# Vision tower on one core: last batch reordered, router logits taken from centred tokens, products with unread results ahead of waits of TensorE

## The chip, the cores and the metric

The kernel runs on one NeuronCore of a Trainium2 chip. The core has a matrix engine (TensorE, PE in the rows), a vector engine (VectorE, DVE), an activation engine (ScalarE, ACT), a general engine (GpSimd, POOL) and a queue for transfers (SyncE, SP). The metric is the device time of one execution in microseconds, the median over several runs.

## What is computed

Eight images of 64 channels x 128 steps x 64 variables pass one transformer layer. All numbers are float32.

```python
h = tok_ref(x, W)                      # rfft of patches, product: (8, 1024, 64)
h = concatenate([cls_tok, h], axis=1)  # one class token ahead of 1024 tokens
h = h + attn(layernorm(h), WQ, WK, WV) # causal softmax attention, head size 64
h = h + ffn(layernorm(h), ...)

def ffn(x, Wr, br, ...):
    feat = mean(x, axis=0)             # over the EIGHT images
    w = softmax(feat @ Wr + br)        # weights of 8 experts for each token place
    h = relu(bn(x @ W1[e] + b1)); h = relu(bn(h @ W2[e] + b2))
    y = h @ Wo[e] + bo                 # three products for each expert
    return sum over e of w[e] * y[e]
```

The layernorm of the second half is (x - mean) / sqrt(var + eps) without gain or offset: a centred token times one number, its rstd. Because the router takes the mean over all eight images, no expert result can be weighted before the last image has passed the attention.

## The kernel before

Batches (images) 0 to 7 go through a software pipeline; every engine has its own program, written out by hand, and semaphores tie them. The order of instructions in each program is the order of the code. Within a batch the attention works on eight tiles of 128 queries. For each tile PE makes the scores (`score`, into the two PSUM banks pairs `Sp[0]`, `Sp[1]`), DVE takes the row minimum of the negated scores (`smax`), ACT the exponential (`expo`), POOL cuts the triangle (`tri`), DVE masks and sums (`mask`), PE transposes (`p_turn`, into `PTB`, whose halves are `PTp[0]` and `PTp[1]`), ACT copies to SBUF (`pt_copy`, semaphore `pt_done`), and PE multiplies with the values (`u_group`, `u_last`, then `o_group` with `WVT`, in the pair `MM`, halves `M0` and `M1`). Batch 7 runs its tiles downwards, 7 to 0.

The tokens' second layernorm is `ln2_centre`, `ln2_sq`, `ln2_ss`, `ln2_rstd`, `ln2_e` for batches 0 to 6 and `last_add`, `last_centre`, `last_sq`, `last_ss`, a rstd on POOL (L569, L571) and `last_e` in two halves A and B for batch 7. `e2_turn` transposes the result and `e2t_copy` brings it to `E2T`, semaphore `e2t_done`. `facc` is the sum of E2T over batches 0 to 6.

`layer1(n)` is the first expert product of pair p = n % 4 of experts in batch n // 4: four products of 64x512. ACT reads it with `h1_wide(n)` (semaphore `h1_done`). There are 32 of them. Numbers 0 and 1 are made in batch 6, numbers 2 to 11 inside the last batch, the rest in the last phase. Those below `NMID` use `PTB`, so that transposes must wait until `h1_wide` has read them; the others alternate between `Sp[0]` and `Sp[1]`.

Behind `layer1(9)` stands the router: facc times `WrB` (L1778), the class token (L1779), E2T of batch 7 times `WrB` (L1785), then on DVE the logits, maximum, difference, on ACT the exponential, on DVE the sum and weights (L1202 to L1228). The class token has a chain of its own (`class_max`, `class_weight`, `class_h`, `class_centre`, `class_ss`, `class_rstd`, then L1768, L1769, L1773 and L1792 on PE). After that comes the last phase: `layer2`, the gating on DVE, `layer3`, `turn_out`, store, batch after batch, from about 288 us to the end.

## Time and profile before

| | us |
|---|---|
| median of 3 runs | 383.86 (382.93 to 384.4) |
| profiled execution, device time | 382.6 |
| its span, first to last instruction | 380.9 |
| PE busy | 356.5 (94% of the span) |
| DVE busy | 270.7 (71%) |
| ACT busy | 199.7 (52%) |
| POOL busy | 133.5 (35%) |
| mean granted TensorE clock | 0.963 of full |

Busy shares alone name PE as the engine to look at. [...] A row of a list in order of time gives the start, the length, the engine, the line of the kernel and the operation with its tiles, count, and in brackets the idle time before it with what ended it. Each float32 product of TensorE appears as two matmul records, each transpose as one; a line's count is of records.

### The profile page before, as it was taken

To read this page: it belongs to the slowest core of one execution; us is meant where nothing else is said; L and a number is where in the kernel's file an instruction comes from. 1 tells how busy PE (TensorE), PEld (TensorE's weight loads), DVE (VectorE), ACT (ScalarE), POOL (GpSimd) and SP (SyncE) were. 2 spreads that over 40 slices of the span, in tenths; PEclk is the share of its full clock that TensorE was granted. 3 is DMA by queue.
4 is the path that set the end of the run, shared out by engine and by line. 5 is a ranking of instruction groups with operands and counts; after the bars stand their busy time and mean duration, and the time that the engine had idled before them with its cause. 6 is when DMAs were issued, how large, how long until landed. Compare 5 with 4: busy or idle time off the path is not lost.

```text
span 380.9 us, 7929 instructions
## 1 busy us (share of the span) xinstructions
PE 356.5 (94%) x2682; PEld 170.9 (45%) x2682; DVE 270.7 (71%) x582; ACT 199.7 (52%) x402; POOL 133.5 (35%) x201
## 2 busy tenths in 40 slices
PE   4889999999999999999999987897999999999985
PEld 2565335356356355355357444352564333333331
DVE  3122867889989989989999989676315566766673
ACT  0224656568468478377387686664535344444410
POOL 7051302525625626626627538315302900000000
PEclk9999999999999999999999999896559999999999
DMA  6999741904605505500000000000000011100112
GB/s 154 224 219 186 147 79 37 186 0 98 128 0 109 113 0 118 102 0 0 2 2 3 0 2 1 2 0 2 1 0 3 2 28 29 29 12 18 29 28 57
DMA packets 28991, 20.44 MB, mean 54 GB/s; under 512 B 12280, under 2 KB 28832, under 8 KB 28960
## 3 DMA queue, kind: packets, MB, share of 16 engines
q1 hardware_dynamic: 28352, 19.91, 25.8%
q8 instruction: 19, 0.31, 0.4%
q10 hardware_dynamic: 608, 0.12, 0.2%
q14 instruction: 12, 0.10, 0.1%
HBM read 17.93 MB, written 2.10 MB: 53 GB/s over the span
## 4 chain that ended last, share of the span: by engine, by line
PE 82%; DVE 5%; issue 4%; ACT 4%; POOL 2%; DMA 1%; SPq 0%; DVEq 0%; POOLq 0%; ACTq 0%
PE Sp L1406 13%; PE Sp L1553 8%; PE MM L1461 6%; PE MM L1687 6%; PE PTB L1418 6%; PE PTB L1665 6%; PE MM L1339 6%; PE MM L1342 5%; PE MM L1469 2%; PE MM L1316 2%; PE Sp L1288 2%; PE MM L1320 2%; PE PTB L1388 1%; POOL st L479 1%; PE Sp L1707 1%
## 5 line engine op out<-in xcount | busy, mean ns | idle before, releaser
L1406 PE MATMUL Sp<-eT,G 64*64 64x512 f32 x512 | 63.7, 599 | 0.2 <-issue 0.2
L449 POOL TENSOR_SCALAR_AFFINE_SELECT EP<-EP 128x128 f32<-128x128 f32 x64 | 23.6, 368 | 103.1 <-ACT EP L654 103.0
L591 ACT ACTIVATE PT<-PTB 128x512 f32<-128x512 f32 (+3 forms) x88 | 38.9, 484 | 26.4 <-PE PTB L1418 23.8
L945 DVE TENSOR_SCALAR_CACHE_REDUCE EP<-Sp,sr 128x1024 f32<-128x1024 f32 x32 | 40.3, 1279 | 5.6 <-PE Sp L1406 5.6
L945 DVE TENSOR_SCALAR_CACHE_REDUCE SN<-Sp,sr 128x1024 f32<-128x1024 f32 x32 | 39.9, 1276 | 1.2 <-PE Sp L1406 1.2
L1406 PEld LDWEIGHTS Sp<-eT,G 64*64 64x64 f32 x512 | 18.8, 133 | 31.4 <-issue 31.2
L1553 PE MATMUL Sp<-E2T,W1f 64*64 64x512 f32 x216 | 31.8, 688 | 0.1
L1461 PE MATMUL MM<-PT,e 128*64 128x512 f32 (+3 forms) x168 | 31.6, 513 | 0.0
L955 DVE SCALAR_TENSOR_TENSOR SN<-SN,EP 128x384 f32<-128x384 f32 (+7 forms) x32 | 27.4, 855 | 4.4 <-ACT EP L657 2.3
L1237 DVE SCALAR_TENSOR_TENSOR EP<-PTB,negc,PTd 128x512 f32<-128x512 f32 x28 | 19.7, 746 | 13.3 <-PE PTB L1665 13.3
L955 DVE SCALAR_TENSOR_TENSOR EP<-EP 128x128 f32<-128x128 f32 (+7 forms) x32 | 27.3, 853 | 2.2 <-ACT EP L657 1.9
L657 ACT ACTIVATE EP<-SN,negm 128x256 f32<-128x256 f32 (+6 forms) x31 | 23.3, 751 | 0.0
L1461 PEld LDWEIGHTS MM<-PT,e 128*64 128x64 f32 x168 | 14.9, 141 | 18.5 <-issue 16.3
L1418 PE MATMUL PTB<-ident,SN 128*128 128x128 f32 x146 | 20.6, 280 | 1.9 <-ACT X L699 1.4
L1418 PEld LDWEIGHTS PTB<-ident,SN 128*128 128x128 f32 x146 | 16.3, 144 | 10.3 <-issue 5.6
L1418 PE MATMUL PTB<-ident,EP 128*128 128x128 f32 x106 | 16.1, 283 | 2.7 <-ACT PTd L591 2.6
L1418 PEld LDWEIGHTS PTB<-ident,EP 128*128 128x128 f32 x106 | 11.4, 142 | 13.8 <-issue 11.2
L591 ACT ACTIVATE UT<-MM 128x512 f32<-128x512 f32 x12 | 7.1, 589 | 18.9 <-PE MM L1687 15.0
L654 ACT ACTIVATE EP<-SN,negm 128x128 f32<-128x128 f32 x32 | 12.8, 400 | 7.6 <-DVE SN L945 7.4
L591 ACT ACTIVATE Z<-MM 128x512 f32<-128x512 f32 x11 | 6.6, 597 | 19.3 <-PE MM L1687 11.7
L657 ACT ACTIVATE EP<-EP,negm 128x128 f32<-128x128 f32 (+6 forms) x25 | 16.6, 662 | 0.0
L479 POOL TENSOR_TENSOR st<-st,cst 128x8 f32<-128x8 f32 x7 | 15.5, 2211 | 1.3 <-POOL st L476 1.3
(334 smaller groups left out, 699.3 us busy)
## 6 DMA issues: line engine op xcount, KB each, us to landing
XW<-in_x_dram SPq DMA_DIRECT2D x6, 1024.0 KB, 10.7
X<-in_x_dram SPq DMA_DIRECT2D x6, 1024.0 KB, 9.5
out_dram<-xc SPq DMA_DIRECT2D x8, 256.0 KB, 2.6
XW<-in_x_dram SPq DMA_DIRECT2D x2, 576.0 KB, 7.9
X<-in_x_dram SPq DMA_DIRECT2D x2, 576.0 KB, 14.2
XW<-in_x_dram SPq DMA_DIRECT2D x2, 448.0 KB, 11.2
X<-in_x_dram SPq DMA_DIRECT2D x2, 448.0 KB, 14.2
EP<-in_L_tok_W_dram SPq DMA_DIRECT2D x2, 144.0 KB, 3.3
```

Of the source, the lines that this page charges most:

```text
L449: pool.affine_select(out=blk_, in_=blk_, compare_op=ALU.is_ge, fill=0.0, base=0, pattern=[[-1, 128]], channel_multiplier=1).then_inc(tri_d ...
L591: return act.activation(dst, src, ACT.Copy)
L657: act.activation(EP[:, p % 2, 0:n], W4[p % 4][:, 0:n], ACT.Exp, bias=negm[q][:, t:t + 1], scale=-1.0).then_inc(left_done, 1)
L945: dve.tensor_scalar(W4[p % 4], Sp[p % 2][:, :], -SCALE, sr[q][:, place(t), 0:1], ALU.mult, ALU.min, accum_out=negm[q][:, t:t + 1]).then_in ...
L955: dve.scalar_tensor_tensor(out=W4[p % 4][:, 0:n], in0=W4[p % 4][:, 0:n], scalar=0.0, in1=EP[:, p % 2, 0:n], op0=ALU.not_equal, op1=ALU.mul ...
L1339: pe.matmul(M0[64 * c:64 * c + 64, :], Wef[:, n, 0, :], X[q][:, :, n, vs], start=(n == 0), stop=False, skip_group_check=True)
L1406: ins = pe.matmul(Sp[p % 2][64 * s:64 * s + 64, CH * c:CH * c + CH], G[q][rows, 128 * t + 64 * s:128 * t + 64 * s + 64], eT[q][rows, :], **ON)
L1418: ins = pe.transpose(PTp[i % 2][:, 128 * k:128 * k + 128], W4[p % 4][:, 128 * (k0 + k):128 * (k0 + k) + 128], ident[:, :])
L1461: ins = pe.matmul(M1[half, q0:CH], e32[q][:, place(k), :], PT[g][:, k, q0:CH], start=(k < 2), stop=(k >= nk - 2), skip_group_check=True)
L1553: ins = pe.matmul(l1_bank(n)[64 * s:64 * s + 64, CH * c:CH * c + CH], W1f[rows, 128 * p + 64 * s:128 * p + 64 * s + 64], E2T[rows, b, :], ...
L1665: ins = pe.matmul(l2_bank(b, p)[c][half:half + 64, :], W2f[rows, p, :], h1[b % 4][rows, c, p, :], **ON)
L1687: ins = pe.matmul(yP[b // (NB - 1)][h][64 * c:64 * c + 64, :], Wof[rows, 2 * j + c, :], t2[b % 2][2 * j + c][rows, :], start=(j == 0), sto ...
```

## The change

1. `keep_up(bank, n)` is new: one product of the 128x128 identity with n columns of E2T, written to a bank whose content is not needed. Nothing reads it. It is called five times: 256 columns in batch 6 between `e_turn_early` and `g_quarters`, 512 in the last batch between `p_turn(b, 0)` and `p_turn(b, 1)`, 512 ahead of the wait for the class token's e2c, 256 ahead of the wait of `e2_turn(b - 1)`, and 384 ahead of the wait for facc.
2. `NMID` goes from 5 to 4: `layer1(4)` is written to `Sp[0]` instead of `PTB`. It waits for `smax` of piece 6 in exchange, since that reads the bank.
3. The program of PE in the last batch: `score` of pieces 6 and 7 ahead of `layer1(3)`; `p_turn` 6 and 7 together ahead of `layer1(5)`; `u_last` both in a row; `layer1(6)` ahead of the layernorm work.
4. The router's logits of batch 7 are made from the centred tokens `xc`: `x_turn` transposes them in two halves (4 transposes together), ACT copies them to `XT` (the tile eT[1]), PE multiplies with `WrB`, and DVE multiplies the 128x64 result with the rstd (`glx`) before it adds. The normalised tokens of batch 7, needed for `layer1(28)` and later only, are made after the logits (`last_e`), transposed by `last_turn` in the last phase behind `layer3(0, 2)`, and copied by ACT after `h1_wide(12)`. `layer1(13)` waits for that copy, since the bank is shared.
5. DVE: `class_arg` and `smax` 6 and 7 come earlier; `ln2_centre(6)` moves from ahead of `mask` 5 to behind `class_centre`, `class_ss` ahead of `last_add` A; `ln2_ss` and `ln2_e` of batch 6 move behind halves A and B; `h1c` of the class token moves ahead of the addition to facc. ACT and POOL follow: `expo` 2, 6 and 7 earlier, `ln2_sq` later, `pt_copy` 6 and 7 ahead of `h1_wide(4)`, `add_up` of half A behind the last `tri`, `class_rstd` ahead of `ln2_rstd`.

PE, from the second product of half A's outputs (UT) to the last product with unnormalised weights. PTB, Sp0, Sp1 and MM are PSUM, SN is the tile with masked exponentials. Before:

```order
L1553 MATMUL PTB<-E2T,W1f 64x512 [waits pt_done,e2t_done]
L1553 MATMUL PTB<-E2T,W1f 64x512 x3
L1418 MATMUL PTB<-ident,SN 128x128 [waits pt_done,p_done,h1_done]
L1418 MATMUL PTB<-ident,SN 128x128
L1553 MATMUL Sp1<-E2T,W1f 64x512 [waits h1_done,e2t_done,negm_done]
L1553 MATMUL Sp1<-E2T,W1f 64x512 x3
L1437 MATMUL MM<-PT0,e32_1 64x384 [waits dve_steps,pt_done]
L1437 MATMUL MM<-PT0,e32_1 64x384
L1437 MATMUL MM<-PT0,e32_1 64x256
L1437 MATMUL MM<-PT0,e32_1 64x128
L1418 MATMUL PTB<-ident,SN 128x128 [waits pt_done,p_done]
L1437 MATMUL Sp0<-PT0,e32_1 64x128 [waits pt_done]
```

After:

```order
L1564 MATMUL Sp0<-E2T,W1f 64x512 [waits h1_done,e2t_done,negm_done]
L1564 MATMUL Sp0<-E2T,W1f 64x512 x3
L1429 MATMUL PTB<-ident,SN 128x128 [waits pt_done,p_done]
L1429 MATMUL PTB<-ident,SN 128x128
L1429 MATMUL PTB<-ident,SN 128x128 [waits pt_done,p_done]
L1448 MATMUL MM<-PT0,e32_1 64x384 [waits dve_steps,pt_done]
L1448 MATMUL MM<-PT0,e32_1 64x384
L1448 MATMUL MM<-PT0,e32_1 64x256
L1448 MATMUL MM<-PT0,e32_1 64x128
L1448 MATMUL PTB<-PT0,e32_1 64x128 [waits pt_done]
L1564 MATMUL Sp1<-E2T,W1f 64x512 [waits h1_done,e2t_done,negm_done]
L1564 MATMUL Sp1<-E2T,W1f 64x512 x3
```

`layer1(4)` (E2T,W1f) left PTB, the transposes behind it lost the wait for h1_done, and both transposes now stand ahead of `u_last` and of `layer1(5)`.

PE, from the class token's first products to the router's last one. Before:

```order
L1773 MATMUL PTB<-e2cT,W1f 128x8 [waits act_steps]
L1773 MATMUL PTB<-e2cT,W1f 128x8 x3
L1553 MATMUL Sp0<-E2T,W1f 64x512 [waits h1_done,e2t_done]
L1553 MATMUL Sp0<-E2T,W1f 64x512 x3
L1778 MATMUL MM<-WrB,facc 128x16 [waits facc_done]
L1778 MATMUL MM<-WrB,facc 128x16 x3
L1779 MATMUL MM<-WrB,f64 128x8
L1477 MATMUL MM<-ident,e32_0 128x128 [waits e2_done]
L1477 MATMUL MM<-ident,e32_0 128x128 x3
L1553 MATMUL Sp1<-E2T,W1f 64x512 [waits h1_done,e2t_done]
L1553 MATMUL Sp1<-E2T,W1f 64x512 x3
L1785 MATMUL MM<-WrB,E2T 128x16 [waits dve_steps,e2t_done]
```

After:

```order
L1406 MATMUL MM<-E2T,ident 128x256
L1488 MATMUL MM<-ident,e232 128x128 [waits e2_done]
L1488 MATMUL MM<-ident,e232 128x128 x3
L1564 MATMUL Sp0<-E2T,W1f 64x512 [waits h1_done,e2t_done]
L1564 MATMUL Sp0<-E2T,W1f 64x512 x3
L1406 MATMUL PTB<-E2T,ident 128x384
L1807 MATMUL PTB<-WrB,facc 128x16 [waits facc_done]
L1807 MATMUL PTB<-WrB,facc 128x16 x3
L1808 MATMUL PTB<-WrB,f64 128x8
L1811 MATMUL MM<-WrB,eT1 128x16 [waits act_steps]
L1811 MATMUL MM<-WrB,eT1 128x16 x3
L1564 MATMUL Sp1<-E2T,W1f 64x512 [waits h1_done,e2t_done]
```

In front of the router stand now products of 256 and of 384 columns whose results are not read, and the transposes of batch 6 (e232). The transposes of batch 7 (e32_0) are gone from here, and the router's second product reads eT1. The transposes of xc stand ahead of these rows, two before the class token's L1796 and two behind it.

PE, in the last batch between the first two groups of transposes. After:

```order
L1429 MATMUL PTB<-ident,EP 128x128 [waits pt_done,p_done]
L1429 MATMUL PTB<-ident,EP 128x128 x3
L1429 MATMUL PTB<-ident,EP 128x128 [waits pt_done,p_done]
L1429 MATMUL PTB<-ident,EP 128x128 x3
L1406 MATMUL MM<-E2T,ident 128x512 [waits e2t_done]
L1429 MATMUL PTB<-ident,EP 128x128 [waits pt_done,p_done]
```

Before, the same rows follow each other without the one from L1406.

```diff
@@ names and steps
+        glx = sb("glx", [128, NT * NEXP])
...
+        XT = eT[1]
...
-        NMID = 5
+        NMID = 4
@@ GpSimd, last_batch
                 tri(b, 5, True)
-                add_up(b, 1, pz, 0)
                 tri(b, 6, True)
                 tri(b, 7, True)
-                ln2_rstd(b - 1)
+                add_up(b, 1, pz, 0)
                 class_h()
                 add_up(b, 0, pzl, 1)
+                class_rstd()
+                ln2_rstd(b - 1)
...
@@ ScalarE, last batch
             pt_copy(b, 0, True)
+            expo(b, 1, 2, True)
             pt_copy(b, 1, True)
-            expo(b, 1, 2, True)
             expo(b, 1, 3, True)
...
+            expo(b, 1, 6, True)
             h1_wide(3)
-
-            ln2_sq(b - 1)
+            expo(b, 1, 7, True)
...
+            pt_copy(b, 6, True)
+            pt_copy(b, 7, True)
             h1_wide(4)
-
-            pt_copy(b, 6, True)
+            act.wait_ge(dve_steps, nth("k_cent", 1))
+            act.activation(e2c[:, :], ccx[:, :], ACT.Square).then_inc(act_steps, 1)
             act.wait_ge(pe_steps, nth("t_ua", 1))
             copy(U2[0][:, 128:CH], M0[:, 128:CH]).then_inc(act_steps, 1)
-            pt_copy(b, 7, True)
             act.wait_ge(pe_steps, nth("t_ub", 1))
-            copy(U2[0][0:64, 0:128], Sp[0][0:64, 0:128]).then_inc(act_steps, 1)
+            copy(U2[0][0:64, 0:128], PTp[0][0:64, 0:128]).then_inc(act_steps, 1)
+            ln2_sq(b - 1)
             h1_wide(5)
...
+            h1_wide(6)
+            act.wait_ge(pe_steps, nth("q_x7", 1))
+            copy(XT[:, 2 * 128:CH], M1[:, 2 * 128:CH]).then_inc(act_steps, 1)
+            last_sq("B", slice(0, QG))
+            act.wait_ge(pe_steps, nth("q_x7", 2))
+            copy(XT[:, 0:2 * 128], M1[:, 0:2 * 128]).then_inc(act_steps, 1)
+            e2t_copy(b - 1, M0)
             h1_wide(7)
             h1_wide(8)
-            e2t_copy(b, M1)
             h1_wide(9)
...
             h1_wide(12)
+            e2t_copy(NB - 1, Sp[1])
@@ VectorE, last batch
+            dve.wait_ge(pool_steps, nth("t_rstdB", 1))
             dve.wait_ge(pe_steps, nth("q_lg", 1))
+            dve.tensor_tensor(glx[:, :].rearrange("p (i c e) -> p i c e", i=QG, c=2),
+                              M1[:, 0:64].rearrange("p (c i e) -> p i c e", i=QG, c=2),
+                              st[:, 3, :].rearrange("p (c i) -> p i c", c=2).unsqueeze(3).to_broadcast([128, QG, 2, NEXP]),
+                              ALU.mult).then_inc(dve_steps, 1)
...
+            last_e(1, A).then_inc(dve_steps, 1)
+            last_e(0, B).then_inc(e2_done, 1)
             dve.wait_ge(pe_steps, nth("c_l2", 1))
@@ TensorE
+            def keep_up(bank, n):
+
+                pe.matmul(bank[:, 0:n], ident[:, :], E2T[:, 0, 0:n], **ON)
...
                 if n == 13:
-                    pe.wait_ge(act_steps, nth("q_bcc", 4))
+                    pe.wait_ge(e2t_done, NB)
...
                 e_turn_early(b + 1, 1 - q)
+                if not y_next:
+                    pe.wait_ge(pt_done, NCH * b + 4)
+                    keep_up(PTp[0], 256)
...
             p_turn(b, 0, paired=True, down=True)
+            pe.wait_ge(e2t_done, b - 1)
+            keep_up(M0, CH)
             p_turn(b, 1, paired=True, down=True)
...
+            def x_turn(x, bank, first, last):
+                for i in range(first, last):
+                    ins = pe.transpose(bank[:, 128 * i:128 * i + 128], x[:, 2 * i:2 * i + 2, :], ident[:, :])
+                ins.then_inc(pe_steps, 1)
+
+            layer1(6)
             pe.wait_ge(dve_steps, nth("t_hA", QG))
-            e2_turn(b - 1, M1)
-            pe.wait_ge(dve_steps, nth("t_hB", QG))
-            layer1(6)
+            keep_up(M1, CH)
             pe.wait_ge(dve_steps, nth("k_e2", 1))
...
             layer1(7)
+            pe.wait_ge(dve_steps, nth("t_hA", QG))
+            x_turn(xc, M1, 2, QG)
             pe.wait_ge(act_steps, nth("q_cmc", 1))
...
+            x_turn(xc, M1, 0, 2)
+            keep_up(M0, 256)
+            e2_turn(b - 1, M0)
             layer1(8)
+            keep_up(PTp[0], 384)
             pe.wait_ge(facc_done, NB)
...
-            e2_turn(b, M1, e2=e32[0])
+            pe.wait_ge(act_steps, nth("q_x7c", 2))
+            for i in range(QG):
+                ins = pe.matmul(M1[:, 16 * i:16 * i + 16], XT[:, 128 * i:128 * i + 128], WrB[:, :], **ON)
+            ins.then_inc(pe_steps, 1)
             layer1(9)
...
                 layer3(b - 1, 2)
+                if b == 1:
+                    last_turn()
                 layer3(b - 1, 3)
```

## Rows read from the trace of the kernel before

**Rows 1.** Page: span, busy time, granted clock in tenths, in 40 slices
```profile
span 380.9 us, 7929 instructions
...
PE 356.5 (94%) x2682; PEld 170.9 (45%) x2682; DVE 270.7 (71%) x582; ACT 199.7 (52%) x402; POOL 133.5 (35%) x201
...
PEclk9999999999999999999999999896559999999999
```

**Rows 2.** Windows: length, busy us of each engine (records), granted clock, DMA, GB/s
```profile
core 0: us, PE busy (x) PEld busy (x) DVE busy (x) ACT busy (x) POOL busy (x), PEclk, DMA share, GB/s
240.15:243.56 3.41, 3.41 (x10) 0.97 (x12) 2.10 (x9) 2.54 (x6) 1.05 (x2) 0.50 0.02 5
260.62:284.52 23.90, 22.98 (x93) 11.17 (x93) 7.90 (x38) 8.99 (x17) 6.61 (x11) 0.50 0.00 1
284.52:288.40 3.88, 3.88 (x47) 2.23 (x46) 1.75 (x10) 2.63 (x4) 0.29 (x1) 1.00 0.02 4
288.40:380.90 92.50, 86.08 (x730) 29.45 (x728) 55.30 (x83) 33.69 (x36) 11.27 (x17) 1.00 0.11 24
```

**Rows 3.** PE in order of time, around the beginnings of two stretches
```profile
235.40 1.09 PE L1418 MATMUL PTB<-ident,EP 128*128 128x128 f32 x8
239.14 1.01 PE L1418 MATMUL PTB<-ident,EP 128*128 128x128 f32 x7 [2.65 <-ACT PTd L591]
...
257.00 1.06 PE L1743 MATMUL MM<-WVT,UT 128*128 128x64 f32 x8
258.57 1.09 PE L1553 MATMUL PTB<-E2T,W1f 64*64 64x512 f32 x8 [0.51 <-ACT PT L591]
261.04 0.69 PE L1418 MATMUL PTB<-ident,SN 128*128 128x128 f32 x2 [1.37 <-ACT X L699]
```

**Rows 4.** PE in order of time, 266 to 284 us
```profile
266.74 0.69 PE L1437 MATMUL Sp<-PT,e 128*64 128x128 f32 x2 [0.37 <-ACT PT L591]
...
270.30 1.99 PE L1553 MATMUL Sp<-E2T,W1f 64*64 64x512 f32 x8
...
274.98 1.87 PE L1773 MATMUL PTB<-e2cT,W1f 64*128 64x8 f32 x8
...
278.69 1.89 PE L1778 MATMUL MM<-WrB,facc 128*128 128x16 f32 x8
...
281.03 1.11 PE L1477 MATMUL MM<-ident,e 128*128 128x128 f32 x4
282.07 1.99 PE L1553 MATMUL Sp<-E2T,W1f 64*64 64x512 f32 x8
```

**Rows 5.** PE in order of time at full clock, elsewhere in the trace
```profile
197.04 0.95 PE L1394 MATMUL MM<-agT,eT 128*128 128x4 f32 x8
...
206.44 0.60 PE L1477 MATMUL Sp<-ident,e 128*128 128x128 f32 x4
...
220.04 1.09 PE L1388 MATMUL PTB<-eT,A 64*64 64x512 f32 x8 [0.88 <-ACT eT L591]
...
370.37 0.66 PE L1697 MATMUL MM<-ident,UT 128*128 128x128 f32 x4 [1.24 <-DVE UT L1242]
...
371.97 3.66 PE L1680 MATMUL Sp<-EP,Wof 128*64 128x512 f32 x16
```

**Rows 6.** DVE and POOL in order of time, batch 7's tokens to logits
```profile
269.01 0.28 DVE L1134 SCALAR_TENSOR_TENSOR H<-MM,pzl,H 128x64 f32<-128x64 f32 x1 [4.01 <-PE MM L1759]
...
277.43 0.42 DVE L1140 TENSOR_TENSOR e<-xc,st 128x256 f32<-128x256 f32 x1
...
285.33 0.22 DVE L1208 SCALAR_TENSOR_TENSOR gl<-MM,gl 128x64 f32<-128x64 f32 x1 [3.96 <-PE MM L1785]
...
274.31 1.01 POOL L571 TENSOR_TENSOR st<-st,cst 128x4 f32<-128x4 f32 x1
```

More of the change, by code:

```diff
@@ L1168, in _ @@
             class_centre()
+            ln2_centre(b - 1)
+            class_ss()
             dve.wait_ge(pvs_done, 2 * b + 1)
@@ L1180, in _ @@
                 last_add(t, pzl, M0[:, D * t:D * t + D])
+            dve.wait_ge(pe_steps, nth("t_ob", 1))
+            last_add(0, pzl, PTp[1][:, 0:D])
             last_ss("A", A)
[L1182 to L1183 removed]
             dve.wait_ge(dve_steps, nth("t_hB", QG))
             last_centre("B", B)
[L1186 removed]
+            ln2_e(b - 1)
             last_ss("B", B)
[L1188 to L1193 removed]
             dve.wait_ge(pe_steps, nth("c_l1", 1))
@@ L1722, in _ @@
             p_turn(b, 3, paired=True, down=True)
+            score(b, 1, 6, True)
             pe.wait_ge(r0_done, NB)
@@ L1744, in _ @@
             ins.then_inc(o_ready, 1)
-            layer1(4, NCH * b + 10)
-            pe.wait_ge(h1_done, 10)
+            pe.wait_ge(negm_done, 8 * NB - 1)
+            layer1(4)
             p_turn(b, 6, paired=True, down=True)
-            pe.wait_ge(negm_done, 8 * NB)
-            layer1(5)
+            p_turn(b, 7, paired=True, down=True)
             pe.wait_ge(pt_done, NCH * b + 11)
@@ L1753, in _ @@
             u_last(QG, M0, 128)
-            p_turn(b, 7, paired=True, down=True)
             pe.wait_ge(pt_done, NCH * NB)
-            u_last(1, Sp[0], 0)
+            u_last(1, PTp[0], 0)
+            pe.wait_ge(negm_done, 8 * NB)
+            layer1(5)
             pe.wait_ge(act_steps, nth("t_uac", 1))
@@ L1825, in _, with last_turn @@
             layer3(0, 1)
+            def last_turn():
+                pe.wait_ge(act_steps, nth("q_bcc", 4))
+                pe.wait_ge(e2_done, NB)
+                for i in range(QG):
+                    ins = pe.transpose(L1p[1][0][:, 128 * i:128 * i + 128], e32[0][:, 2 * i:2 * i + 2, :], ident[:, :])
+                ins.then_inc(e2t_ready, 1)
             for b in range(1, NB):
```

82 lines of the change are left out of this document (32 added, 50 removed).

## The prediction

> **What bounds the kernel now.** I read three views in this order. The page first [rows 1]: PE is busy 94% of the span, so time is won where PE works slowly or stands still. The row of the granted clock names the place: it is full nearly everywhere and falls to 6, 5, 5 tenths near the end of the attention. [...] In the long stretch it was busy 22.98 of 23.90 us while DVE was busy 7.90, ACT 8.99 and POOL 6.61. So this stretch is bound by PE at half clock. From 288.40 to the end PE is busy 86.08 of 92.50 us at full clock, and this last phase begins only when the router is through: what PE reaches sooner in the stretch, the end reaches sooner.
>
> The list in order of time shows what PE did before each fall [rows 3]. Before the first it stood idle 2.65 us between two groups of transposes. Before the second it had 1.06 us of products with 64 columns, 0.51 us idle, one `layer1` of 1.09 us, and 1.37 us idle. PE then fed on little for long: the class token's products with 8 columns (1.87 us) and the router's with 16 (1.89 us), with `layer1` between them [rows 4]. The clock came back only at 284.5, behind transposes and a `layer1` in a row.
>
> **Does half the clock mean twice the time?** The same work stands in the trace at both clocks. `layer1` takes 1.99 us [rows 4]; the four 64x512 products of L1388 take 1.09 with the drain of the last one [rows 5]. Four transposes take 1.11 against 0.60, four products with few columns 1.89 against 0.95 [rows 4, 5]. So work scales by about two, idle time does not. At full clock the busy part of the stretch would be 22.98 / 2 = 11.5 us: a saving of 11.5. [...]
>
> **The long stretch, part by part.**
> - Waits. `layer1(4)` no longer waits for a half of PTB (0.51), `p_turn(6)` no longer for `h1_wide(4)` (1.37) [rows 3], and `u_last` of one tile no longer for a lone copy (0.37) [rows 4]: 2.25 us. In exchange `p_turn` 6 and 7 now stand back to back ahead of `u_last`, which needs the copy of the first; nothing covers that copy but one transpose. I leave 0.5 us for it. Gain 1.75, bounds 1.2 and 2.2. That these waits go is the first reason for the clock to stay: the 1.9 us idle of [rows 3] shrink to some 0.5.
> - Products with unread results, three in this region: 512 + 256 + 384 = 1152 columns. The nearest row is L1680 with 128 rows: 8 products of 512 columns, two at a time, in 3.66 us [rows 5], so 0.91 for one that fills the array. 1152 / 512 x 0.91 = 2.1 us at full clock. Do they lie in waits? If PE runs at full clock and is behind, they do not: from the additions of half A (about 262) e2c needs some 1.5 us of DVE and POOL, while PE has `u_last`, two `layer1` and the outputs, over 4 us, ahead of it; the copy of E2T that facc needs has `layer1(8)` as cover. I take the whole 2.1 as cost; bound below 0.5, if the chains are slower than I think.
> - Router from centred tokens. New: four transposes (0.60 [rows 5]) and two small copies on ACT, which has the time. The four transposes of the normalised tokens leave this stretch and come back in the last phase at the same 0.6, where PE has no gap at that place. Net cost 0.6. The dependency that this shortens (POOL's rstd ended at 275.3, `last_e` waited behind the class token until 277.43, the logits' addition came at 285.33 [rows 6]) was not the limit: DVE stood waiting for PE 3.96 us before it. At full clock it would be one, and this edit takes it away; that is its worth, and it is inside the halving above.
> - DVE: one more operation of the size of the additions to the logits (0.22 us [rows 6]), behind `layer1(9)` and two more; hidden. `last_e` moved behind the logits adds 0.84 us of DVE before the weights. The exponential on ACT and PE's `layer1` 10, 11 and `layer2` cover it: cost 0, and at most 0.4.
> - `ln2_centre(6)` (1.6 us) now sits between `class_centre` and the additions of half A on DVE. The half-B products of PE, which DVE waited for by 4.01 us [rows 6], come later than that work even at full clock. Cost 0; up to 1 if DVE runs late.
>
> Sum: -11.5 - 1.75 + 2.1 + 0.6 = -10.6 us.
>
> **The rest.** The 512-column product at 236.5 lies in the 2.65 us of idle [rows 3] and the 256-column one in the 0.88 us before L1388 [rows 5]: both wait there for ACT, so they cost nothing as time. Their worth is the first fall. It slowed 3.41 us of busy PE, so 1.7 us are to be had, since scores come next and DVE waits for them. The idle left is 2.65 - 0.9 = 1.75 us. Gaps of 0.88 and 1.24 us left the clock at full [rows 5], 1.37 + 0.51 with little work between ended in a fall. The value lies between 0 and 1.7; 1.75 is nearer the fall, but it is now preceded by a dense product. I take 0.8. The move of `score` 6 and 7 ahead of `layer1(3)` changes the order, not the sum, and feeds DVE sooner.
>
> Total -11.4. The profiled execution took 382.6, 1.3 below the median of 383.86, so it would give 371.2 and the median 383.86 - 11.4 = **372.5 us**.
>
> **Rivals.**
> 1. *The clock falls again for a short time.* The router's products (facc, class token, batch 7) now follow each other: 0.95 + 0.3 + 0.95 us with 8 or 16 columns, then one `layer1`, then the class token's second product. It is the thinnest place of the new order, and in the old trace the clock did not come back over just such work. For it: the old fall came with thin products plus idle; against: here no idle is left. One fall like that at 240.15 costs 1.7 us, two 3.4: 374.2 to 375.9.
> 2. *The clock falls at the class token's products and stays down until after the router.* Between `layer1(7)` and `layer1(9)` lie about 6.3 us of work at full clock with the two unread products; at half it takes 12.6. That gives 378.8. [...]
> 3. *DVE, ACT or POOL becomes the bound.* At full clock PE is 11 us faster and the layernorm chain of batch 7 with 1.6 us of `ln2_centre` ahead is next. If it leaves PE waiting some 3 us in all, partly in place of the unread products: 375.5.
> 4. *The clock does not hold at all (the slower side).* The fall at 260.6 comes in spite of shorter waits, and the unread products run at half clock: 2 x 2.1 = 4.2, the new transposes 1.1, one set of transposes moves to full clock (-0.5), waits -1.75. Sum +3.0: 386.9. With a share f of the stretch at full clock the change wins 11.5 f - 2.7 (2 - f) + 1.75; it turns to a loss below about f = 0.26.
>
> **How the numbers follow.** Forecast, long stretch gone and the first fall gone or not (371.6 to 373.4, with the bounds of waits and unread products 370 to 374.5): 0.57. Rival 1: 0.17. Rival 2: 0.10. Rival 3: 0.06. Rival 4: 0.10. The range goes from 370.0 to 378.0; it takes in rivals 1 and 3 and leaves out 2 and 4. A measurement of this kernel can tell about 0.5% (1.9 us) from no change. Faster by more: all but rival 4 and a tail of rival 2, 0.88. Within: 0.03, the tails of both. Slower: 0.09, the rest of rival 4.
>
> **What would show it.** The granted clock at 1.00 from 244 us to the end; `layer1` 5 to 9 at about 1.1 us each instead of 1.99; no wait of PE for `h1_wide` between 257 and 262; the gating of batch 0 beginning about 10 us sooner; the distance from there to the end longer by 0.6. If the clock is at 0.50 for more than 4 us behind 257, rival 1, 2 or 4 holds, by its length. If the clock is full and PE waits more than 1 us at L1788 or L1807 of the new kernel, rival 3. Wrong altogether would be a stretch at full clock without a shorter time to the last phase.

## The result, and the profile after

The changed kernel takes **371.29 us** (median of 4 runs, 369.55 to 373.43) beside 384.13 us of the kernel before in the same set (382.93 to 384.67). The ratio is 0.967, 95% interval 0.962 to 0.973: 12.8 us less by the medians. Ratios here and below leave out executions more than 1.5% above the fastest of the same kernel; medians leave out none. The profiled execution took 371.4 us against 382.6, 11.2 us less.

The page of the changed kernel: span, busy time, and the granted clock in 40 slices.

```profile
span 369.6 us, 7961 instructions
...
PE 348.3 (94%) x2696; PEld 167.9 (45%) x2696; DVE 270.8 (73%) x583; ACT 199.9 (54%) x404; POOL 132.8 (36%) x201
...
PEclk9999999999999999999999999999999999999999
```

Against [rows 1], the 6, 5, 5 in the row of the clock are gone. PE's busy share is 94% as before, at a mean granted clock of 1.000 where it was 0.963: the busy share did not show the clock, the row below it does. DVE, ACT and POOL did the same work in both.

The windows of the changed kernel, cut so that each answers to one of [rows 2] (columns as there). Its pair of 240.15:243.56 stands at nearly the same place; 256.20:277.50 holds what took half the clock before; the last begins behind the router.

```profile
240.15:243.56 3.41, 3.41 (x23) 1.47 (x25) 2.95 (x10) 2.65 (x6) 1.51 (x3) 1.00 0.02 5
256.20:277.50 21.30, 20.43 (x162) 10.71 (x161) 12.39 (x55) 14.00 (x26) 7.70 (x14) 1.00 0.01 2
277.50:369.60 92.10, 86.03 (x727) 29.41 (x727) 55.03 (x83) 33.18 (x36) 11.27 (x17) 1.00 0.11 24
```

In the first window PE has 23 matmul records where it had 10 before, in the same 3.41 us, busy throughout in both; some of the 23 are shorter ones of the work behind `u_group`.

PE in order of time, from batch 6 to the first transposes of the outputs in the last phase; these answer to [rows 3 to 5]. L1406 is `keep_up`, L1564 `layer1`, L1429 the transposes, L1472 `u_group`, L1826 the transposes of the weights, with which the last phase begins.

```profile
197.09 0.95 PE L1401 MATMUL MM<-agT,eT 128*128 128x4 f32 x8
...
236.38 1.02 PE L1406 MATMUL MM<-E2T,ident 128*128 128x512 f32 x2
239.19 1.01 PE L1429 MATMUL PTB<-ident,EP 128*128 128x128 f32 x7 [1.79 <-ACT PTd L593]
240.13 3.01 PE L1472 MATMUL MM<-PT,e 128*64 128x512 f32 x16
...
255.62 1.06 PE L1759 MATMUL MM<-WVT,UT 128*128 128x64 f32 x8
256.61 1.09 PE L1564 MATMUL Sp<-E2T,W1f 64*64 64x512 f32 x8
257.63 0.55 PE L1429 MATMUL PTB<-ident,SN 128*128 128x128 f32 x3
258.54 1.08 PE L1448 MATMUL MM<-PT,e 128*64 128x384 f32 x7 [0.36 <-ACT PT L593]
...
262.84 1.12 PE L1406 MATMUL MM<-E2T,ident 128*128 128x512 f32 x2
...
265.76 1.05 PE L1796 MATMUL PTB<-e2cT,W1f 64*128 64x8 f32 x8
...
267.02 0.60 PE L1406 MATMUL MM<-E2T,ident 128*128 128x256 f32 x2
267.45 0.60 PE L1488 MATMUL MM<-ident,e 128*128 128x128 f32 x4
...
269.00 0.91 PE L1406 MATMUL PTB<-E2T,ident 128*128 128x384 f32 x2
269.75 0.96 PE L1807 MATMUL PTB<-WrB,facc 128*128 128x16 f32 x8
...
276.40 0.66 PE L1826 MATMUL MM<-ident,gwp 128*128 128x128 f32 x4
...
296.81 0.66 PE L1711 MATMUL MM<-ident,UT 128*128 128x128 f32 x4
```

The idle time ahead of the first fall is 1.79 us where it was 2.65, and `u_group` behind it takes 3.01 us. `layer1(4)` waits for nothing. Up to 277.5 us two waits are left, 0.36 us for the copy of `p_turn` and 0.17 us ahead of `layer1(11)`; a `layer1` takes 1.09 us. The class token's 8-column products take 1.05 instead of 1.87, facc's 16-column ones 0.96 instead of 1.89.

Before going on, one reading of the numbers that all runs share. Each execution comes with its mean granted clock. A time multiplied by that clock is about the time with the loss at half speed taken off. An execution with a share s at half clock has the mean 1 - s/2 (before: 27.31 us [rows 2] and 0.8 us at the end, of 380.9, give 0.963), and it loses about s/2 of its time if all of its work takes twice as long there (`layer1` 1.99 us against 1.09). It is an estimate, since it counts idle time at half clock as lost too, and it scatters: over 12 executions of the changed kernel it gives 369.3 to 371.7 us. The kernel before, 33 executions in three sets: medians of 369.7, 370.0 and 370.3 us. The changed kernel, those 12 executions in two sets: 370.6 and 370.4 us. **By this estimate the two kernels would take the same time at full clock, within 1 us.** What the change gained is the clock. What it saved in waits (1.9 us) it spent on unread products (2.0) and on item 4 (0.8), as the runs below show.

### The profile page after: what moved, and what is told of

Same layout as the page of the kernel before. It is cut to its first block, busy times and chain, and to the rows that moved or that the text cites. A ratio compares the mean times of both kernels' runs of the same rounds, so it can differ in the third digit from the quotient of the medians.

```text
span 369.6 us, 7961 instructions
## 1 busy us (share of the span) xinstructions
PE 348.3 (94%) x2696; PEld 167.9 (45%) x2696; DVE 270.8 (73%) x583; ACT 199.9 (54%) x404; POOL 132.8 (36%) x201
## 4 chain that ended last, share of the span: by engine, by line
PE 80%; DVE 4%; issue 4%; DMA 4%; ACT 3%; POOL 2%; SPq 1%; DVEq 0%; POOLq 0%; ACTq 0%
PE Sp L1417 13%; PE Sp L1564 7%; PE MM L1701 7%; PE PTB L1679 7%; PE PTB L1429 6%; PE MM L1472 6%; PE MM L1346 6%; PE MM L1349 5%; DMA XW<-in_x_dram 4%; PE MM L1480 3%; PE MM L1323 2%; PE PTB L1395 1%; PE MM L1327 1%; POOL st L481 1%; PE Sp L1721 1%
## 5 line engine op out<-in xcount | busy, mean ns | idle before, releaser
L1472 PE MATMUL MM<-PT,e 128*64 128x512 f32 (+3 forms) x168 | 29.9, 491 | 0.0
L1564 PE MATMUL Sp<-E2T,W1f 64*64 64x512 f32 x224 | 28.6, 602 | 0.2 <-ACT XW L701 0.2
L1472 PEld LDWEIGHTS MM<-PT,e 128*64 128x64 f32 x168 | 14.5, 137 | 17.2 <-issue 15.1
L1429 PE MATMUL PTB<-ident,SN 128*128 128x128 f32 x146 | 19.9, 277 | 0.6 <-ACT PTd L593 0.6
L1429 PEld LDWEIGHTS PTB<-ident,SN 128*128 128x128 f32 x146 | 16.2, 143 | 8.1 <-issue 5.6
L1429 PE MATMUL PTB<-ident,EP 128*128 128x128 f32 x106 | 16.1, 282 | 1.9 <-ACT PTd L593 1.8
L656 ACT ACTIVATE EP<-SN,negm 128x128 f32<-128x128 f32 x32 | 12.8, 401 | 9.1 <-DVE SN L950 7.4
L1429 PEld LDWEIGHTS PTB<-ident,EP 128*128 128x128 f32 x106 | 11.4, 142 | 13.5 <-issue 10.9
L469 POOL TENSOR_TENSOR H<-H,ot 128x256 f32 (+1 forms) x14 | 14.0, 997 | 3.2 <-DVE ot L990 1.9
```

The source lines that it names most:

```text
L1429: ins = pe.transpose(PTp[i % 2][:, 128 * k:128 * k + 128], W4[p % 4][:, 128 * (k0 + k):128 * (k0 + k) + 128], ident[:, :])
L1472: ins = pe.matmul(M1[half, q0:CH], e32[q][:, place(k), :], PT[g][:, k, q0:CH], start=(k < 2), stop=(k >= nk - 2), skip_group_check=True)
L1564: ins = pe.matmul(l1_bank(n)[64 * s:64 * s + 64, CH * c:CH * c + CH], W1f[rows, 128 * p + 64 * s:128 * p + 64 * s + 64], E2T[rows, b, :], ...
```

## The experiments

Twelve runs of ten different kernels stand in three sets, each set on one chip beside 11 executions of the kernel before. Times are medians (lowest to highest); the mean granted clock of the executions is given as a range, with the number of executions at 0.995 or less. Above that, the end of the span alone can account for what lacks: the profiled execution of `layer1(4)` in PTB, at 0.996, has the full clock to 366 us and half from 366.8 to 369.6. At 0.995 I take it as open: the profiled execution without all five has 3.41 us at half, at 241.01, and none at its end.

| kernel | us | clock of its executions | 0.995 or less |
|---|---|---|---|
| set 1: before | 383.42 (380.77 to 387.13) | 0.958 to 0.972 | 11 of 11 |
| changed kernel | 370.93 (370.21 to 373.55) | 0.990 to 1.000 | 1 of 6 |
| without product of the gap | 373.46 (371.46 to 374.35) | 0.988 to 0.993 | 6 of 6 |
| without the late three | 371.29 (368.24 to 371.78) | 0.988 to 1.000 | 4 of 6 |
| without all five | 371.95 (370.44 to 374.18) | 0.979 to 0.995 | 6 of 6 |
| set 2: before | 381.72 (380.67 to 386.89) | 0.958 to 0.972 | 11 of 11 |
| before + product of the gap | 379.65 (372.15 to 384.41) | 0.963 to 0.999 | 5 of 6 |
| before + all five | 375.6 (373.29 to 380.31) | 0.975 to 0.997 | 5 of 6 |
| router from normalised tokens | 369.6 (369.08 to 370.34) | 0.996 to 1.000 | 0 of 6 |
| thin products apart | 369.95 (368.08 to 373.6) | 0.983 to 0.998 | 3 of 6 |
| set 3: before | 380.95 (376.15 to 385.1) | 0.962 to 0.985 | 11 of 11 |
| changed kernel | 371.84 (370.02 to 375.49) | 0.984 to 1.000 | 3 of 6 |
| `layer1(4)` in PTB | 374.32 (371.27 to 376.45) | 0.986 to 0.997 | 4 of 6 |
| router from normalised tokens | 369.95 (369.43 to 372.08) | 0.995 to 0.999 | 1 of 6 |
| the same, two products less | 370.35 (368.59 to 374.79) | 0.986 to 1.000 | 3 of 6 |

**My theory** after the result: the order with its shorter waits ends the long stretch at half clock, the product in the gap ends the short one, and the late products are the price of holding the clock over the router. **The rivals**: the unread products do it all, the order nothing; the order does it all, the products nothing; and the shorter chain over rstd has a part in it.

### Changed kernel again

> The changed kernel as it is, as the yardstick for the three that are run with it on the same chip. Expected 371.3 us (369.5 to 373.5), 12 to 13 below the kernel before, the granted clock at 1.00 from 12 us to the last product.

370.93 us, ratio 0.970 (0.965 to 0.974). In set 3 it stood beside a faster kernel before:

> The changed kernel without an edit, as the yardstick of this set of runs. 371 us (369.6 to 373.6 in the runs so far), TensorE's granted clock at full from 11 us to the end, its waits behind 250 us 0.4 (p_turns on ScalarE), 0.6 (l1_turn on ScalarE) and 0.2 us.

371.84 us, ratio 0.979 (0.974 to 0.984). The profiled execution was the slowest of its six, 375.49 us. Three windows of it, of two stretches at half clock and of the one ahead of the second:

```profile
33.85:40.67 6.82, 6.82 (x32) 3.09 (x27) 2.85 (x6) 1.22 (x6) 0.29 (x1) 0.50 0.72 117
272.77:276.19 3.42, 3.42 (x45) 2.78 (x48) 1.43 (x7) 1.13 (x2) 0.00 (x0) 1.00 0.02 5
276.19:279.61 3.42, 3.42 (x22) 1.46 (x18) 1.46 (x9) 2.30 (x3) 0.29 (x1) 0.50 0.01 2
```

So the clock can still fall in the changed kernel, in some executions. By distances between the same instructions in the traces of this run and of the result, the first stretch cost 3.2 us (12.00 against 8.80 around it) and the second 1.3 (22.08 against 20.78 from the products of UT to the weights), together 4.5; 375.49 - 4.5 = 371.0, where the executions at clock 1.0 have 371.33 and 371.37. The second fall stands out: PE was busy 3.42 of 3.42 us ahead of it, with the router's products of 16 and 8 columns, those of the class token and a `layer1`.

### Without the product in the gap

```diff
-            pe.wait_ge(e2t_done, b - 1)
-            keep_up(M0, CH)
```

> The changed kernel without the 512-column product between the first two groups of transposes of the last batch; all else stays. Theory 1 (that product alone keeps the clock over the gap at 237 us): the idle time there goes back from 1.79 to 2.65 us, the clock falls for about 3.4 us as in the kernel before, +1.7 us against the changed kernel, some 373.0. Rival (the clock stays because the neighbouring work is arranged otherwise): no fall, same time as the changed kernel within 0.3 us. Both expect the clock at 1.00 from 256 us on.

373.46 us against 370.93. PE around the gap, and the window behind it:

```profile
239.47 1.01 PE L1429 MATMUL PTB<-ident,EP 128*128 128x128 f32 x7 [2.64 <-ACT PTd L593]
240.41 4.71 PE L1472 MATMUL MM<-PT,e 128*64 128x512 f32 x16
```

```profile
240.45:243.86 3.41, 3.41 (x9) 0.96 (x10) 2.94 (x10) 2.27 (x5) 1.52 (x3) 0.50 0.02 5
```

The idle time is 2.64 us again, and `u_group` takes 4.71 us. All six executions have a clock below 0.994, which fits a fall every time; the place of it is seen in the profiled one. One product of 512 columns, in time in which PE waited anyway, removed it. By the trace it is worth 4.71 - 3.01 = 1.7 us; by the medians 2.5, with ranges that allow either.

### Without the three late products

```diff
-            keep_up(M1, CH)
-            keep_up(M0, 256)
-            keep_up(PTp[0], 384)
```

> The changed kernel without the three unread products (512, 256, 384 columns) behind layer1(6), ahead of the transposes of batch 6 and ahead of the product with facc. Theory 1 (the reordering and the shorter waits hold the clock, the three products are pure cost): clock at 1.00 throughout, PE reaches the last phase 1.9 us sooner, some 369.4. Theory 2 (they are needed at the thin place): the clock falls once or for long between 265 and 275 us, +1.7 to +6 minus the 1.9 saved, so 371 to 375. Theory 3 (they lie in waits of PE anyway): clock full, but new waits of together 1 to 2 us, time unchanged.

371.29 us, ratio 0.967 (0.962 to 0.971), against 370.93, 0.970: no difference that can be told. But the six times fall apart: two at clock 1.0 took 368.24 and 368.59, three at 0.988 took 371.71 to 371.78. The profiled execution is of the second kind. PE in order of time, and the window:

```profile
267.13 1.07 PE L1804 MATMUL PTB<-WrB,facc 128*128 128x16 f32 x8 [0.40 <-DVE facc L1202]
...
268.44 1.21 PE L1808 MATMUL MM<-WrB,eT 128*128 128x16 f32 x8
269.58 1.99 PE L1564 MATMUL Sp<-E2T,W1f 64*64 64x512 f32 x8
```

```profile
269.22:276.05 6.83, 6.83 (x47) 3.42 (x50) 2.74 (x13) 2.65 (x4) 0.29 (x1) 0.50 0.00 1
```

This is my rival 1, at the place that it named: facc, class token and batch 7 in a row, and the clock falls in the third group. It costs 6.83 / 2 = 3.4 us. With the products that fall is avoided and they cost about 2.2. The two come out even in the median. Fewer executions lack clock with the products (1 of 6 against 4 of 6), but the times are no steadier: both kernels' times spread over some 3.4 us. The clock fell behind 2.65 us of idle at the first gap before, and here at 269.22 with no wait longer than 0.40 us near it: short gaps alone did not protect it.

### Without all five unread products

> The changed kernel without any of the five unread products. If their effects add up: the first fall is back (+1.7) and the rest as in the run without the three late ones: with theory 1 there 371.1, with theory 2 there 373 to 377. If the clock falls at 260 us for as long as in the kernel before, it is the products and not the order that held it: 380 or more.

371.95 us, ratio 0.972 (0.967 to 0.977). The diff is the sum of the two before and the 256-column product of batch 6. The windows of its first fall and of the old long stretch's work:

```profile
241.01:244.42 3.41, 3.41 (x11) 1.04 (x9) 2.58 (x10) 1.91 (x5) 1.51 (x2) 0.50 0.02 5
256.20:277.50 21.30, 20.37 (x174) 11.51 (x170) 13.48 (x65) 15.16 (x28) 9.29 (x16) 1.00 0.01 2
```

So the new order, with the router from centred tokens, is enough to end the long stretch in this execution, and by the medians it brings about 11.5 of the 12.5 us that the whole change won in this set. The other clocks go down to 0.979, so some executions had further time at half, at places that no trace shows.

### The old order with the product in the gap

> The kernel before with one thing added: the unread product of 512 columns between the first two groups of transposes of the last batch. Theory (it alone holds the clock over that gap): no fall at 240 us, the long fall at 260 us as before but beginning and ending 1.7 us sooner; 383.4 - 1.7 = 381.7 us. If the effect needed the rest of the change: the fall stays, 383.4.

379.65 us against 381.72 by the medians, 2.1 less where 1.7 was expected; with single executions 12 us apart that proves little, and the trace has to carry it. `keep_up` was added to the kernel before, with one call. Its profiled execution (381.24 us) has no fall at 240, as the theory says, and the long one is cut in two:

```profile
258.83:262.24 3.41, 3.41 (x15) 0.90 (x16) 2.53 (x14) 0.37 (x1) 1.93 (x5) 0.50 0.00 0
262.24:269.07 6.83, 4.33 (x34) 2.30 (x34) 3.40 (x16) 4.61 (x10) 1.58 (x4) 1.00 0.00 1
269.07:286.14 17.07, 17.07 (x90) 10.01 (x90) 3.31 (x16) 5.96 (x8) 2.49 (x4) 0.50 0.00 1
```

The clock came back, PE then waited 2.5 of 6.83 us, and it fell again, for 17.07 us with PE busy all the time. The fall begins 4.52 us behind the start of the products of UT (254.31 here), where in the kernel before it is 3.62 (260.62 - 257.00 in [rows 2, 3]); PE's instructions from there on are the same. The executions of this one kernel reach from 372.15 us at 0.999 to 384.41 at 0.963. So the length of the long fall is no property of the order alone. Whether the edit 20 us earlier moved it in the profiled execution, or something that differs from execution to execution, cannot be told from one trace of each.

### The old order with all five products

```diff
+                if not y_next:
+                    pe.wait_ge(pt_done, NCH * b + 4)
+                    keep_up(PTp[0], 256)
...
+            pe.wait_ge(e2t_done, b - 1)
+            keep_up(M0, CH)
...
+            keep_up(M1, 256)
             e2_turn(b - 1, M1)
...
+            keep_up(M0, CH)
             pe.wait_ge(dve_steps, nth("k_e2", 1))
...
+            keep_up(M0, 384)
             pe.wait_ge(facc_done, NB)
```

> The kernel before in its own order, with five unread products: 256 columns in batch 6 and 512 in the first gap as in the change, and 256 ahead of the transposes of batch 6, 512 ahead of the class token's products, 384 ahead of facc. Theory 1 (the long fall comes from PE's waits of 0.51 and 1.37 us, which stand ahead of the late products): the fall at about 259 us stays, the late products run at half clock (+4.1), the first gap gives -1.7: 385.8 us. Theory 2 (more dense work lets the clock come back sooner in the stretch): the stretch at 0.50 is some 7 us shorter, 380 to 382.

375.6 us, ratio 0.982 (0.977 to 0.986). Theory 1 of this run, that the fall stays long, is wrong in the profiled execution and by the clocks of four more; one, at 0.975 and 380.31 us, is near the kernel before. PE at the waits that the new order removes and at the first of the late products, and the windows:

```profile
259.02 1.09 PE L1557 MATMUL PTB<-E2T,W1f 64*64 64x512 f32 x8 [0.52 <-ACT PT L591]
261.48 0.44 PE L1422 MATMUL PTB<-ident,SN 128*128 128x128 f32 x2 [1.38 <-ACT X L699]
...
267.88 0.65 PE L1399 MATMUL MM<-E2T,ident 128*128 128x256 f32 x2
```

```profile
261.97:265.38 3.41, 3.41 (x15) 0.89 (x16) 2.53 (x14) 0.37 (x1) 1.93 (x5) 0.50 0.00 0
265.38:281.00 15.62, 14.52 (x116) 8.32 (x116) 5.94 (x28) 9.49 (x16) 3.79 (x6) 1.00 0.01 2
```

With both waits in place the clock fell behind the second one, as before, but it was back after 3.41 us and held over the router. The return at 265.38 is not the work of the late products, since the first of them starts at 267.88; the run with the gap product alone had the same return after 3.41 us. What differs is what follows. There PE waited 1.07 and 0.92 us more and the clock fell again at 269.07; here unread products stand in that place, 0.59 us of wait is left, and it held. By the medians the order alone brings 11.5 us (371.95 in set 1) and the products alone 6.1 (375.6 in set 2); they leave the waits and the short fall. What ends the first 3.41 us at half in these two traces, and not in the kernel before, is not shown.

### Thin products apart

The late products are left out, and batch 7's logits stand ahead of `layer1(8)`, away from facc's and the class token's.

```diff
-            keep_up(M1, CH)
...
-            keep_up(M0, 256)
             e2_turn(b - 1, M0)
+            pe.wait_ge(act_steps, nth("q_x7c", 2))
+            for i in range(QG):
+                ins = pe.matmul(M1[:, 16 * i:16 * i + 16], XT[:, 128 * i:128 * i + 128], WrB[:, :], **ON)
+            ins.then_inc(pe_steps, 1)
             layer1(8)
-            keep_up(PTp[0], 384)
```

> The changed kernel without the three late unread products, and with the logits of batch 7 (four products of 16 columns) moved ahead of layer1(8), so that thin work no longer stands in one piece behind layer1(8). If the fall at 269 us of the run without the three products came from the piece of 2.2 us of thin products in a row: clock full in all executions, 368.4 (the level of that kernel's executions at clock 1.00). If any lack of dense work between 262 and 273 us is enough: the fall comes elsewhere, 370 to 372.

369.95 us, ratio 0.972 (0.966 to 0.977): three executions at 368.1 to 368.9 with a clock of 0.996 or more, three at 371.0 to 373.6 with 0.983 to 0.991. Moving the thin products apart did not hold the clock in all executions either. The profiled one had the full clock up to 365 us and gives the **price of the late products** in the trace. PE from an instruction of batch 6 (`MM<-agT,eT`, in both kernels alike) to the transposes of the weights:

```profile
196.68 0.95 PE L1401 MATMUL MM<-agT,eT 128*128 128x4 f32 x8
...
273.98 0.66 PE L1823 MATMUL MM<-ident,gwp 128*128 128x128 f32 x4
```

77.30 us against 276.40 - 197.09 = 79.31 in the changed kernel: the three products cost 2.0 us, if the moved logits cost nothing, and cover next to nothing.

### `layer1(4)` back in PTB

```diff
-        NMID = 4
+        NMID = 5
...
-            layer1(4)
+            layer1(4, NCH * b + 10)
+            pe.wait_ge(h1_done, 10)
...
+            h1_wide(4)
             pt_copy(b, 6, True)
             pt_copy(b, 7, True)
-            h1_wide(4)
```

> The changed kernel with one part of the reordering undone: layer1(4) writes PTB again and so stands behind h1_wide(4) of ScalarE, as in the kernel before; everything else, the five unread products too, stays. At full clock the wait of PE for h1_wide should come back at about 257 us with 0.5 to 1.4 us. Theory 1 (this wait is what lets the clock fall at 260): the clock falls to half within 5 us behind it, but the unread products let it back after 3.4 to 7 us; 371 + 1.0 (wait) + 1.7 to 3.4 (work at half) = 374 to 375.5 in the executions in which it falls. Theory 2 (the order of the later steps and the products hold the clock, the wait alone does not matter): the clock stays at full and only the wait is added, 372 to 372.5. Theory 3 (the wait moves to where PE would have waited anyway): 371, as the yardstick.

374.32 us against 371.84. PE in the profiled execution, the fastest of the six (371.27), and a window behind it:

```profile
257.55 0.55 PE L1429 MATMUL PTB<-ident,SN 128*128 128x128 f32 x3 [1.38 <-ACT X L701]
```

```profile
260.00:277.40 17.40, 16.92 (x136) 8.95 (x128) 8.34 (x35) 11.66 (x19) 5.07 (x7) 1.00 0.01 2
```

The old wait is back, 1.38 us where [rows 3] have 1.37, and here the clock stayed full behind it (theory 2). The distance from `MM<-agT,eT` to the weights is 276.32 - 195.56 = 80.76 us, 1.45 more than the changed kernel. So this wait need not bring the fall, and it takes its own 1.4 us. In the other executions the clock is 0.986 to 0.997; whether it fell behind this wait or elsewhere their records do not say. The median is 2.5 us above the changed kernel's, of which the wait explains 1.4, and four executions lie at 374.28 to 376.45, as theory 1 has it. That theory is refuted for the profiled execution and open for these.

### Router from normalised tokens

The fourth item of the change undone, everything else kept (`last_e` ahead of the class token, one `e2_turn` of batch 7 ahead of `layer1(9)`, no `XT`, no `glx`, no `last_turn`). The core of it, on PE:

```diff
-            pe.wait_ge(act_steps, nth("q_x7c", 2))
-            for i in range(QG):
-                ins = pe.matmul(M1[:, 16 * i:16 * i + 16], XT[:, 128 * i:128 * i + 128], WrB[:, :], **ON)
-            ins.then_inc(pe_steps, 1)
-            layer1(9)
+            e2_turn(b, M1, e2=e32[0])
+            layer1(9)
+            pe.wait_ge(e2t_done, NB)
+            for i in range(QG):
+                ins = pe.matmul(M1[:, 16 * i:16 * i + 16], E2T[:, b, 128 * i:128 * i + 128], WrB[:, :], **ON)
+            ins.then_inc(pe_steps, 1)
```

> The changed kernel with the router taken back to normalised tokens: last_e ahead of facc, transposes of batch 7 behind the product with f, copy to E2T by ScalarE under layer1(9), logits behind layer1(9); no transposes of xc, none in the last phase. Order of the last batch and all five unread products stay. As predicted (at full clock the chain over the rstd becomes the limit): PE waits 1 to 2 us for it, 372 to 373. Rival (the chain has room even at full clock, the edit is worth nothing): 370.9, or 370.3 since four transposes fewer.

369.6 us in set 2. The second time it stood beside the changed kernel:

> The changed kernel with the router computed from the normalised tokens again, as in an earlier run, now beside the yardstick on one chip, because the earlier 369.6 us was beside another set of runs of the kernel before. If the centred tokens only cost (four more transposes of 0.6 us in sum, and the extra operations of VectorE and ScalarE), this one is 0.6 to 1.3 us below the yardstick, 369.6 to 370.4. If the earlier gap was the chip's and not the kernel's, the two are within 0.4 us. If the chain over rstd is a limit in part of the executions, this one is slower by up to 1 us.

369.95 against 371.84 us; time by clock 369.1 against 370.4. PE's waits between 234 and 292 us (total, times, longest), and DVE at the place where my prediction put the limit:

```profile
PE PTB L1420 <- ACT PTd L593: 2.4, 2, 1.8
PE Sp L1712 <- ACT EP L593: 0.6, 1, 0.6
PE MM L1439 <- ACT PT L593: 0.4, 1, 0.4
```

```profile
267.12 0.43 DVE L1141 TENSOR_TENSOR e<-xc,st 128x256 f32<-128x256 f32 x1 [0.57 <-POOL st L573]
...
272.22 0.23 DVE L1206 SCALAR_TENSOR_TENSOR gl<-MM,gl 128x64 f32<-128x64 f32 x1 [2.37 <-PE MM L1799]
```

PE waits for nothing at the router. DVE had the normalised tokens at 267.6 us, and 4.7 us later it still stood waiting for PE, by 2.37 us: at full clock the chain over rstd is as little a limit as at half. What the item costs, by the same distances:

```profile
196.09 0.95 PE L1392 MATMUL MM<-agT,eT 128*128 128x4 f32 x8
...
275.30 0.66 PE L1813 MATMUL MM<-ident,gwp 128*128 128x128 f32 x4
...
294.98 0.66 PE L1702 MATMUL MM<-ident,UT 128*128 128x128 f32 x4
```

79.21 us to the weights against 79.31 of the changed kernel, and from there to the first transposes of the outputs 19.68 against 20.41 (296.81 - 276.40). 0.1 + 0.7 = 0.8 us, which buy nothing. **The version without item 4 has the lowest median in both of its sets and the narrowest spread**; the interval of its ratio in set 3, 0.970 to 0.980, still overlaps that of the changed kernel.

### The same with two products less

```diff
-            keep_up(M1, CH)
             pe.wait_ge(dve_steps, nth("k_e2", 1))
...
-            keep_up(M0, 256)
```

> As router_normalised_again, and without the unread products ahead of the class-token products and ahead of e2_turn (512 and 256 columns, 0.91 + 0.46 = 1.4 us at full clock); the one of 384 columns ahead of x_l1 stays. If the clock holds without them, 1.0 to 1.4 us below router_normalised_again, 368.3 to 369; if it falls among the thin products of the router, as in the run without the three late products, for 3.4 to 6.8 us of which 1.7 to 3.4 are lost, 370 to 371.5; with some executions of either kind, a median between and a wider spread.

370.35 us: three executions at 368.59 to 369.26 with a clock of 1.0, one at 371.44, two at 374.7 and 374.79 with 0.986. The profiled one is of the last kind:

```profile
268.54 1.07 PE L1791 MATMUL PTB<-WrB,facc 128*128 128x16 f32 x8 [1.17 <-DVE facc L1200]
```

```profile
266.60:270.04 3.44, 2.27 (x14) 1.61 (x15) 1.10 (x3) 1.74 (x2) 0.83 (x1) 1.00 0.00 0
270.04:280.28 10.24, 10.24 (x60) 5.27 (x59) 1.91 (x11) 4.38 (x5) 0.29 (x1) 0.50 0.01 2
```

One wait of 1.17 us for facc ahead of the thin products, and 10.24 us at half clock, about 5.1 us lost. The three executions at clock 1.0 win some 0.8 us over the version with both products; the falls in the other three take more than that back, and the median gains nothing.

## Why the prediction was right, and where its steps were not

The forecast was 372.5 us, the time is 371.29, inside the range and on the side named. That it lies this near is in part luck: errors of both signs cancel, as the terms below show. The distances on PE, between the same instructions in both traces, let each step be set beside the term that it had. Two rows of the kernel before, besides [rows 3], the transposes of the weights and the first transposes of the outputs:

```profile
288.41 0.66 PE L1799 MATMUL MM<-ident,gwp 128*128 128x128 f32 x4
...
308.09 0.66 PE L1697 MATMUL MM<-ident,UT 128*128 128x128 f32 x4
```

- **The halving.** Forecast -11.5. The old stretch is 23.90 us at 0.50 from 260.62, with PE busy for 22.98 [rows 2]. From the products of UT to the weights the changed kernel needs 276.40 - 255.62 = 20.78 us, the old one 288.41 - 257.00 = 31.41: 10.6 less for all steps of this region, where my terms, without the 0.6 of the last phase, gave 11.5 + 1.75 - 2.1 = 11.15. The mechanism was right, the sum 0.5 too large. What I halved does not quite halve: `layer1` 1.99 to 1.09, the class token's products 1.87 to 1.05, four transposes 1.11 to 0.60, facc's products 1.89 to 0.96, so 0.02 to 0.12 us too much was taken for each group, over some twenty groups. I take that for most of the 0.5. With the other terms as measured (-1.9, +2.0, +0.1), the halving itself is 10.8 where 11.5 was forecast.
- **Waits.** Forecast -1.75. The 0.51, 1.37 and 0.37 us are gone, and 0.36 stands in front of `u_last`: -1.9. That the shorter waits are the first reason for the clock to stay is the half of the step that the runs do not bear out: with 1.38 us of wait back the clock held in the profiled execution, and in the old order with all waits it came back after 3.41 us, ahead of the first late product. So the stretch ended as forecast, but not for a reason that is shown.
- **Unread products.** Forecast +2.1 in full as a cost. Measured +2.0 by the distances; 2.2 by their starts (262.84, 267.02 and 269.00, with 1.05, 0.43 and 0.75 us until the next instruction). That was right. The forecast did not say that they pay for themselves: without them the trace has a fall that costs about 3.4 us, and three of six executions have the clock of that trace.
- **The router.** Forecast +0.6 net, measured +0.7 in the last phase and +0.1 before it. The step that failed is the sentence that at full clock the chain over rstd would be the limit and that this edit takes it away, with its worth inside the halving. The run without it has no wait of PE there and the full clock. I had divided PE's times by two and left DVE's and POOL's where they stood in the old trace; but they stood so late because they were waiting for PE (4.01 us ahead of the additions, [rows 6]). Their place moved up with PE.
- **First fall.** Forecast -0.8, a middle between 0 and 1.7; it was the full 1.7 in the traces. The idle time left, 1.79 us, was as forecast (1.75), and the product ahead of it was enough.
- **DVE and `ln2_centre`.** Forecast 0: no new wait of PE for DVE in the trace. Right.
- **The rivals.** Rival 1, at 0.17, happens at its place without the late products. In the changed kernel single executions lack clock, 373.43, 373.55, 373.58 and 375.49 us at 0.984 to 0.995; the one trace of these has a fall just behind the router's products, at 276.19, and a longer one far away, at 33.85. Rival 2's 12.6 us at half were in no trace of the new order; the nearest is 10.24 us with two products less. Rival 3 did not come: PE waited 0.36 and 0.17 us. Rival 4 was far off: with the old waits in place and the products added there was still a gain.

The profiled executions were forecast 11.4 apart; they are 11.2 apart, and their spans 11.3. Up to the first gap nothing changed (239.14 - 197.04 = 42.10 us in [rows 3, 5], 239.19 - 197.09 = 42.10 after). From there to the products of UT 17.86 us became 16.43: 1.7 from the first fall, less 0.3, which the new order of `score` and `layer1` costs and to which I had given nothing. Then -10.6, and +0.7 in the last phase (296.81 - 276.40 = 20.41 against 308.09 - 288.41 = 19.68). So 0.5 too much in the long stretch and 0.3 not foreseen stand against 0.9 too little at the first fall; that these nearly cancel is luck. The median came 12.8 lower, since the kernel before was 1.5 slower in that set's median than in its profile.

Left open: what in the new order keeps the clock. `layer1(4)` alone was not it in the one trace; `score` 6 and 7 ahead of `layer1(3)`, the two `p_turn` together and `layer1(6)` ahead of the layernorm were not tried one by one. Open too is why one kernel's executions differ in clock; the profiles show the falls of one execution each, the mean clock of the others tells only how much.

## What to carry to other kernels

Read the row of the granted clock before the busy share, multiply times by their mean clock, and see whether an edit won work or clock: here PE's share was 94% in both kernels, and the medians of time by clock were 369.7 to 370.3 us before and 370.4 and 370.6 after, so it was all clock. A product with an unread result was free where the engine waited anyway (the two groups of transposes around the gap start 3.74 us apart with it and without it), and it was worth its place there, 1.7 us by the trace, since without it all six executions lacked clock. In the engine's path the three late ones cost 2.0 us and have to be weighed against a fall of some 3.4 us that came in some executions only. When PE got faster, the chains that waited for it moved up with it: DVE's last operation on the normalised tokens began at 267.12 us with the router from normalised tokens, where it was 277.43 before. So don't shorten such a chain before a wait shows.

## What the runs showed of the hardware

- The same kernel got different clocks from execution to execution, on one chip: 0.963 to 0.999, 384.41 to 372.15 us, in the old order with one product in the gap. One profiled execution is a sample of that; the clocks of the six executions say whether some time at half is always there (gap product off: all six at 0.993 or less) or at times (late products off: three at 0.988, two at 1.0).
- A fully busy PE did not hold the full clock: it fell at 276.19 us behind 3.42 us busy of 3.42, with products of 16 and 8 columns and a `layer1` (changed kernel, 375.49 us), and in the old order with the gap product it stayed at half for 17.07 us with PE busy for all of it, with products of 8 and 16 columns, of 64 rows, and four transposes. In the profiled execution of the same order with products of 128 rows and 256 to 512 columns between them the clock stayed full from 265.38 us on.
- Two profiled executions, of the changed kernel and of the old order with all five products, were at half clock for 6.8 us from 33 us on, far ahead of anything that was edited on PE; the profiled executions of the result and of set 1 were not. At 3.2 us such a fall is as large as most of the edits.
- Half of the time at half clock was lost roughly, but not always, where PE was busy all through: 3.41 us at half made `u_group` 1.70 us longer (4.71 against 3.01), 6.82 us from 33.85 us cost 3.2, but the 3.42 us from 276.19 cost 1.3.
